# Projections of q and k made whole in every second batch, in place of halves in neighbouring batches

## The chip, the cores and the metric

The kernel runs on one core of one Trainium2 chip. The metric is the device time of one execution in microseconds; the time before is 4257.07 us, the median of 3 runs (4256.78 to 4263.16).

## The reference

The input is x of shape (8, 512, 32, 32): 8 images, 512 channels, 1024 tokens. Everything is fp32.

```python
def _mhsa(x, w_qkv, b_qkv, w_o, b_o):          # 8 heads of 64
    t = x.reshape(B, C, H * W).transpose(0, 2, 1)
    q, k, v = jnp.split(t @ w_qkv + b_qkv, 3, axis=-1)     # then split into heads
    scores = jnp.einsum('bhnd,bhmd->bhnm', q, k) / jnp.sqrt(jnp.float32(hd))
    out = jnp.einsum('bhnm,bhmd->bhnd', jax.nn.softmax(scores, axis=-1), v)
    return (out @ w_o + b_o)                   # back to (B, C, H, W)
def layer(x):                                  # x is the group norm of the input
    p = sigmoid(relu(mean(x, (2, 3)) @ w1 + b1) @ w2 + b2)
    m = (p > 0.5)[:, :, None, None]
    hyp = _logmap0(_mhsa(_expmap0(x * m), *hdn_weights))
    euc = _mhsa(x * (1 - m), *eu_weights)
    return hyp + euc
out = x + layer(_gn(x))
```

`_expmap0` and `_logmap0` scale each row of 32 numbers along the last axis by a function of its norm.

## The kernel before, in words

The kernel loops over the 8 images, and in each image over two passes, t = 0 (the first weight set, hdn) and t = 1 (the second, eu). A pass is the attention of four pairs of heads. It is cut into 32 batches of two steps each; a step is 128 keys of one pair against 512 queries. Five engines each walk through the same 32 batches in an order written out by hand, and wait for one another at semaphores that count what was made.

On TensorE, batch b is (lines 1284 to 1305): the maximum slot M0 (`max_slot`, two matmuls, L1184, into banks 0 and 1), the scores of two steps (`scores`, L1232, 16 matmuls in four parts each of high and low halves), the maximum slot M1, the products of the two steps before with v (`prob_v`, L1246), in batches 5, 9, 13, ... the denominators (`denominator`, L1256), in batches 7, 15, 23, 31 the negated row maxima turned by a matmul with the identity (`neg_rows`, L1193), and then `project(b)`: the projections that `projections(b)` (L103) lists for this batch. In pass 1, batches 2, 3, 5 and 6 have small tiles of the gate for the next image as well (`gate_tile`, L1142 to L1153); in batch 5 the one called hidden stands behind the projection and waits for a VectorE result (L968).

The maximum slots compute q times k of the next pair a second time, so that the row maxima of the softmax are known before its scores are. Both matmuls of a slot write banks 0 and 1, and VectorE reduces them (`max_slot` of VectorE, L1034, 128x1024). The next slot writes the same two banks, so M1 of a batch waits for the reduction of its M0, and M0 of the next batch for that of M1.

The projections make q and k of the pairs ahead. A tile (p, k) is one 128x512 half of q or k of pair p (p of 4 and 5 are pairs 0 and 1 of the next pass); it takes 12 matmuls L1135 (four blocks of channels, each high by high, high by low, low by high), accumulated in bank 2. `done` is the batch in which the tile gets complete: 4, 6, 8, ... 30, and 32 for the last two, which is the tail of the pass. Before the change, the first 6 matmuls stand in batch done - 1 and the other 6 in batch done; two tiles, (4, 0) in batch 20 and (5, 3) in batch 32, are whole. When a tile is complete, ScalarE writes its high part (`qk_hi`, L747) at the end of batch done, and VectorE its low part (`qk_lo`, L1023) in the batch behind, between its reductions of M0 and M1. v tiles (12 matmuls each) are made in batches 0 to 3, two in each, ahead of the tiles of q and k.

VectorE's order in batch b is (lines 1097 to 1113): the reduction of M0, the low part of the tile made in batch b - 1, the reduction of M1, then one half of a reciprocal of denominators (L1072, even batches from 6 to 30, and 31), in batches 11, 15, 19, 23, 27 and 31 the low part of the attention's output (`o_lo`, L1077), and `operand_step` (L961). That one has work in pass 1 alone (as has `y_scale_step` in its batches 0 to 2): statistics, norms of rows (L971), in batch 13 a chain of some 15 small operations on scales (L901 to L910 and others), and in batches 15 to 22 the multiply of a chunk of the next operand by its scales (L995), which waits for ScalarE's mask (L695).

GpSimd sums the probabilities of the steps (L640, 128x1024, seven in each eight steps), multiplies the output by the reciprocals (L647) and makes the low part of the next operand (L614). SyncE issues the loads; the weights w_qk of pair p for q or k are loaded once the last tile that reads the old ones is complete.

Of the kernel before, what the change touches and what calls it, by code (L numbers as in the profile page):

```python
# [18 lines left out]
PAIRS = HEADS // 2  # L19
# [83 lines left out]
def projections(b):  # L103

    out = [("v", m) for m in (2 * b, 2 * b + 1) if m < NT]
    for p in range(2, PAIRS + 2):
        for k in range(4):
            done = min(8 * p + QK_AT[k], BATCHES)

            first = done if (p, k) in ((PAIRS, 0), (PAIRS + 1, 3)) else done - 1  # L110
            out += [("qk", p, k, part) for part in range(2) if b == (first, done)[part]]
    return out


def made(b):

    return [f[:3] for f in projections(b) if f[0] == "v" or f[3]]
# [22 lines left out]
def aux_tiles(t):  # L140
# [18 lines left out]
    for b in range(BATCHES):  # L159
        for j in range(2):  # L160
            out += maxima(*max_slot_at(b, j))
        if phase_at(b, DEN) is not None:
            out += [((t, "den", phase_at(b, DEN)), "A", (1,))]
        if neg_pair(b) is not None:
            out += neg(neg_pair(b))
        gate = [((t, GATE_BATCH[b]), "D", (0,))] if t == 1 and b in GATE_BATCH else []
        if b != 5:
            out += gate
        for f in projections(b):
            if f[0] == "v":  # L170
                out += [((t,) + f, "A", (LAST_SCORE if f[1] % 2 else 1 if f[1] == 6 else 2,))]
            elif f[3]:
                out += [((t,) + f[:3], "Q", (2,))]
        if b == 5:
            out += gate
# [16 lines left out]
def build(nc, x, w1, b1, w2, b2, hw_qkv, hb_qkv, hw_o, hb_o, ew_qkv, eb_qkv, ew_o, eb_o, out):  # L192
    ctx = ExitStack()
    with ctx:
# [930 lines left out]
        def _(pe):  # L1125
# [82 lines left out]
            with pe.Fori(0, B) as i:  # L1208
                for t in range(2):
# [67 lines left out]
                    def project(b):  # L1277
                        for f in projections(b):
                            if f[0] == "qk":
                                qk_tile(i, t, f[1], f[2], (f[3],))  # L1280
                            else:
                                v_tile(f[1])
# [56 lines left out]
```

## Time and profile before

| | |
|---|---|
| median of 3 runs | 4257.07 us |
| the profiled execution | 4255.99 us, its span 4254.2 us |
| TensorE busy | 4027.7 us, 95% of the span, 21822 matmuls |
| VectorE busy | 2613.5 us, 61% |
| ScalarE busy | 1949.8 us, 46% |
| GpSimd busy | 2696.1 us, 63% |
| mean granted clock of TensorE | 0.982 |

The page gives the busy time of each engine and the chain of work that ended last. A wait on an engine that is not on that chain costs nothing. In the rows below PE is TensorE, DVE is VectorE, ACT ScalarE and POOL GpSimd; aux_ps holds banks 0 to 2.

### The profile page before, as it was taken

The numbers are of one execution on the slowest core, as the hardware profiler recorded it, in microseconds if no ns is written. First come the engines' busy times: TensorE is split into PE (matmuls) and PEld (weight loads), VectorE is DVE, ScalarE is ACT, GpSimd is POOL, SyncE is SP. The second block draws the span as 40 slices with busy tenths as digits, with TensorE's granted clock in tenths as the row PEclk, the third lists the DMA queues.
The fourth block names the chain that finished last, engine by engine and source line by source line (L and its number), as shares of the span: only waits on it lengthen the run. The fifth ranks groups of instructions, "written<-read, shape, count | busy, mean of one in ns | idle before, by whom it ended". The sixth has DMA issues, their size and how long they took to land.

```text
span 4254.2 us, 69112 instructions
## 1 busy us (share of the span) xinstructions
PE 4027.7 (95%) x21822; PEld 2420.4 (57%) x21822; DVE 2613.5 (61%) x2747; ACT 1949.8 (46%) x3520; POOL 2696.1 (63%) x1311
## 2 busy tenths in 40 slices
PE   4999899998999989998999999999899998999989
PEld 3556465564656546565565655656556564565645
DVE  5465845668465674667746577365763657646585
ACT  4454534545355443544535445354453544435353
POOL 4683766747675575755758458584585836858367
PEclk9999999999999999999999999999999999999999
DMA  7112131121211213121131211212112121121212
GB/s 264 65 41 95 53 100 45 48 96 42 95 55 57 91 33 110 41 77 65 39 104 45 82 55 51 93 53 75 57 61 85 53 88 46 62 90 41 92 51 85
DMA packets 143726, 306.49 MB, mean 72 GB/s; under 512 B 17248, under 2 KB 30048, under 8 KB 133088
## 3 DMA queue, kind: packets, MB, share of 16 engines
q1 hardware_dynamic: 143328, 301.53, 21.1%
q8 instruction: 207, 3.39, 0.3%
q14 instruction: 191, 1.56, 0.1%
HBM read 251.15 MB, written 50.33 MB: 71 GB/s over the span
## 4 chain that ended last, share of the span: by engine, by line
PE 84%; DVE 8%; issue 4%; DMA 2%; ACT 1%; POOL 0%; SPq 0%; DVEq 0%; ACTq 0%
PE aux_ps L1135 29%; PE acc_ps L1246 21%; PE score_ps L1232 20%; PE aux_ps L1184 8%; PE score_ps L1135 3%; PE aux_ps L1256 2%; DVE mxp L1034 2%; DMA xin<-in_x_dram 1%; DVE sc L902 1%; PE aux_ps L1193 1%; DVE sc L909 1%; DVE sc L910 0%; DVE small L903 0%; DVE sc L901 0%; DMA probs<-in_L_conv_eu_w_o_dram 0%
## 5 line engine op out<-in xcount | busy, mean ns | idle before, releaser
L640 POOL TENSOR_TENSOR sums<-sums,probs 128x1024 f32<-128x1024 f32 x768 | 1867.9, 2432 | 887.2 <-ACT probs L811 846.9
L1034 DVE TENSOR_REDUCE mxp<-aux_ps 128x2 f32<-128x1024 f32 x1031 | 1262.4, 1224 | 1204.0 <-PE aux_ps L1184 1192.8
L811 ACT ACTIVATE probs<-score_ps 128x512 f32<-128x512 f32 x2048 | 1057.2, 603 | 662.7 <-PE score_ps L1232 654.9
L1246 PE MATMUL acc_ps<-probs,v_y 128*64 128x512 f32 x4096 | 1015.9, 617 | 0.0
L1135 PE MATMUL aux_ps<-xs,w_qk 128*128 128x512 f32 x3072 | 835.4, 410 | 0.0
L1135 PEld LDWEIGHTS aux_ps<-xs,w_qk 128*128 128x128 f32 x3072 | 546.1, 189 | 412.1 <-issue 296.8
L640 POOL TENSOR_TENSOR sums<-probs 128x1024 f32<-128x1024 f32 x128 | 305.6, 2387 | 474.2 <-ACT probs L811 474.2
L1184 PE MATMUL aux_ps<-k_hi,q_hi 64*128 64x512 f32 x2062 | 474.2, 453 | 138.2 <-DVE mxp L1034 133.3
L1246 PEld LDWEIGHTS acc_ps<-probs,v_y 128*64 128x64 f32 x4096 | 252.0, 138 | 479.8 <-issue 442.1
L1072 DVE RECIPROCAL den<-den 128x256 f32<-128x256 f32 (+1 forms) x240 | 444.0, 1850 | 7.7 <-ACT den L822 7.7
L1232 PE MATMUL score_ps<-q_hi,k_hi 64*128 64x512 f32 x2048 | 408.5, 394 | 18.8 <-issue 18.8
L1184 PEld LDWEIGHTS aux_ps<-k_hi,q_hi 64*128 64x128 f32 x2062 | 199.1, 186 | 371.3 <-DVE mxp L1034 176.6
L1232 PE MATMUL score_ps<-q_hi,k_lo 64*128 64x512 f32 x2048 | 407.1, 393 | 0.0
L1232 PE MATMUL score_ps<-q_lo,k_hi 64*128 64x512 f32 x2048 | 406.8, 392 | 0.0
L1232 PE MATMUL score_ps<-q_max,first_row 64*128 64x512 f32 x2048 | 406.5, 392 | 0.0
L1135 PE MATMUL aux_ps<-o_t,w_o 128*128 128x512 f32 x1536 | 356.5, 391 | 0.2
L1135 PEld LDWEIGHTS aux_ps<-o_t,w_o 128*128 128x128 f32 x1536 | 286.4, 188 | 75.2 <-issue 16.3
L747 ACT ACTIVATE k_hi<-aux_ps,bias_q 128x512 fp32r<-128x512 f32 x128 | 88.1, 689 | 373.6 <-PE aux_ps L1135 373.6
L1077 DVE SCALAR_TENSOR_TENSOR o_t<-o_raw,bias_q,o_t 128x512 fp32r<-128x512 f32 x128 | 188.0, 1469 | 109.4 <-ACT o_t L827 109.4
L647 POOL TENSOR_TENSOR o_raw<-o_raw,den 128x512 f32<-128x512 f32 x128 | 169.5, 1324 | 133.1 <-DVE den L1072 133.1
L1232 PEld LDWEIGHTS score_ps<-q_hi,k_hi 64*128 64x128 f32 x2048 | 194.0, 186 | 47.8 <-issue 24.5
L1232 PEld LDWEIGHTS score_ps<-q_max,first_row 64*128 64x128 f32 x2048 | 195.3, 186 | 44.3
(142 smaller groups left out, 3441.9 us busy)
## 6 DMA issues: line engine op xcount, KB each, us to landing
w_qk<-w_split SPq DMA_DIRECT2D x130, 512.0 KB, 4.2
xin<-in_x_dram SPq DMA_DIRECT2D x256, 256.0 KB, 2.9
w_o<-w_split SPq DMA_DIRECT2D x32, 1024.0 KB, 7.2
w_v<-w_split SPq DMA_DIRECT2D x32, 1024.0 KB, 6.1
v_y<-in_x_dram SPq DMA_DIRECT2D x72, 256.0 KB, 2.9
y<-v_y SPq DMA_DIRECT2D x64, 256.0 KB, 2.0
xin<-y SPq DMA_DIRECT2D x64, 256.0 KB, 2.8
out_dram<-v_y SPq DMA_DIRECT2D x64, 256.0 KB, 7.1
```

The source lines that it names most:

```text
L640: pool.tensor_tensor(sums[h][:, :], a, probs[:, g % SLOTS_P, :], ALU.add).then_inc(c_sum[h].sem, 1)
L647: pool.tensor_tensor(o_raw[:, ph % 2, :], o_raw[:, ph % 2, :], den[:, ph % 2, :], ALU.mult).then_inc(c_on.sem, 1)
L747: act.activation((q_hi, k_hi)[what][:, p % 2, token_half(h)], ps, ACT.Identity, bias=bias_q[:, tt, what, pp:pp + 1]).then_inc(c_hi.sem, 1)
L811: act.activation(probs[:, n % SLOTS_P, token_half(u % 2)], score_ps[:, u % SCORE_BANKS, :], ACT.Exp, scale=SCALE).then_inc(c_exp.sem, 1)
L1034: dve.tensor_reduce(mxp[:, :, n, h], ps, AX.X, ALU.max).then_inc(c_free["D"].sem, 1)
L1072: dve.reciprocal(den[:, ph % 2, first:last], den[:, ph % 2, first:last]).then_inc(c_rec.sem, parts[1] - parts[0])
L1077: dve.scalar_tensor_tensor(o_t[:, 1, p, token_half(h)], o_raw[:, ph % 2, :], bias_q[:, t, 2, p:p + 1], o_t[:, 0, p, token_half(h)].bitcast ...
L1135: last = nc.tensor.matmul(ps, lhs(a, k), rhs(b, k), start=(j == 0), stop=(j == len(todo) - 1))
L1184: last = nc.tensor.matmul(ps[:, j, :], q_hi[head(j), p % 2, n * P:(n + 1) * P], k_hi[head(j), p % 2, token_half(h)], start=True, stop=True)
L1232: last = nc.tensor.matmul(score_ps[:, (2 * n + j) % SCORE_BANKS, :], lhs, qq[head(j), p % 2, cols], start=(s == 0), stop=(s == 3))
L1246: last = nc.tensor.matmul(acc_ps[head(j), :], v_y[:, m, head(2 * p + j)], probs[:, n % SLOTS_P, token_half(j)], start=(m == 0), stop=(m == ...
L1256: last = nc.tensor.matmul(ps[head(j), :], ones[:, :], sums[h][:, token_half(j)], start=True, stop=True)
```

## The change

The list of projections puts both halves of each tile of q and k into batch `done`. So batches 5, 7, 9, ... 31 and 3 hold no matmuls of q or k any more, and batches 4, 6, 8, ... 30 hold 12 of them in place of 6; the tail of the pass (batch 32) makes (5, 2) and (5, 3) whole. The tiles, their banks, the order in which they get complete, and all other engines' programs are as before.

```diff
@@ -106,8 +106,7 @@
     for p in range(2, PAIRS + 2):
         for k in range(4):
             done = min(8 * p + QK_AT[k], BATCHES)
-
-            first = done if (p, k) in ((PAIRS, 0), (PAIRS + 1, 3)) else done - 1
+            first = done
             out += [("qk", p, k, part) for part in range(2) if b == (first, done)[part]]
     return out
```

## Rows read from the trace of the kernel before

**Rows 1.** Section 4 of the page: shares of the chain that ended last, by engine.
```profile
PE 84%; DVE 8%; issue 4%; DMA 2%; ACT 1%; POOL 0%; SPq 0%; DVEq 0%; ACTq 0%
```

**Rows 2.** Waits of TensorE: who, for whom; us in total, times, longest.
```profile
PE aux_ps L1184 <- DVE mxp L1034: 133.3, 62, 8.6
```

**Rows 3.** Timeline (start, us, what) of TensorE, pass 0, end of batch 14, batch 15.
```profile
1240.84 1.67 PE L1135 MATMUL aux_ps<-xs,w_qk 128*128 128x512 f32 x6
1242.44 0.50 PE L1184 MATMUL aux_ps<-k_hi,q_hi 64*128 64x512 f32 x2
...
1244.62 0.39 PE L1184 MATMUL aux_ps<-k_hi,q_hi 64*128 64x512 f32 x2
...
1246.81 0.70 PE L1193 MATMUL aux_ps<-ident,mxw 128*65 128x128 f32 x8
1247.34 1.60 PE L1135 MATMUL aux_ps<-xs,w_qk 128*128 128x512 f32 x6
1248.87 0.50 PE L1184 MATMUL aux_ps<-k_hi,q_hi 64*128 64x512 f32 x2
```

**Rows 4.** The same of batches 19 and 20 and the start of batch 21.
```profile
1267.64 0.50 PE L1184 MATMUL aux_ps<-k_hi,q_hi 64*128 64x512 f32 x2
...
1272.00 0.50 PE L1184 MATMUL aux_ps<-k_hi,q_hi 64*128 64x512 f32 x2
...
1275.11 0.49 PE L1184 MATMUL aux_ps<-k_hi,q_hi 64*128 64x512 f32 x2 [0.74 <-DVE mxp L1034]
1275.53 1.94 PE L1246 MATMUL acc_ps<-probs,v_y 128*64 128x512 f32 x8
1277.40 3.01 PE L1135 MATMUL aux_ps<-xs,w_qk 128*128 128x512 f32 x12
1280.35 0.50 PE L1184 MATMUL aux_ps<-k_hi,q_hi 64*128 64x512 f32 x2
```

**Rows 5.** Timeline of VectorE, end of batch 19 and start of batch 20.
```profile
1271.39 2.44 DVE L1077 SCALAR_TENSOR_TENSOR o_t<-o_raw,bias_q,o_t 128x512 fp32r<-128x512 f32 x1
1273.75 1.21 DVE L1034 TENSOR_REDUCE mxp<-aux_ps 128x2 f32<-128x1024 f32 x1
```

**Rows 6.** Timeline of GpSimd in the same stretch.
```profile
1270.89 2.39 POOL L640 TENSOR_TENSOR sums<-sums,probs 128x1024 f32<-128x1024 f32 x1
```

**Rows 7.** Timelines of VectorE and TensorE, pass 1, batch 16 and what leads to it.
```profile
1517.51 1.21 DVE L1034 TENSOR_REDUCE mxp<-aux_ps 128x2 f32<-128x1024 f32 x1
...
1515.65 0.50 PE L1184 MATMUL aux_ps<-k_hi,q_hi 64*128 64x512 f32 x2
1518.87 0.49 PE L1184 MATMUL aux_ps<-k_hi,q_hi 64*128 64x512 f32 x2 [0.86 <-DVE mxp L1034]
```

**Rows 8.** Timeline of VectorE, pass 0, batch 11.
```profile
1221.49 1.87 DVE L1077 SCALAR_TENSOR_TENSOR o_t<-o_raw,bias_q,o_t 128x512 fp32r<-128x512 f32 x1
```

**Rows 9.** Windows of GpSimd, batches 17 to 19: window, us, busy (instructions), clock, DMA.
```profile
1257.55:1273.28 15.73, 15.57 (x8) 1.00 0.30 100
```

**Rows 10.** Timeline of TensorE, pass 1, the hidden gate tile in batch 5.
```profile
1439.36 0.82 PE L1150 MATMUL aux_ps<-small,xin 128*128 128x1 f32 x6 [1.17 <-DVE small L968]
```

**Rows 11.** Timeline of VectorE, pass 1, batches 11 and 12.
```profile
1477.15 2.42 DVE L1077 SCALAR_TENSOR_TENSOR o_t<-o_raw,bias_q,o_t 128x512 fp32r<-128x512 f32 x1
...
1480.09 1.21 DVE L1034 TENSOR_REDUCE mxp<-aux_ps 128x2 f32<-128x1024 f32 x1
```

**Rows 12.** Timeline of TensorE, pass 1, M1 of batch 14.
```profile
1503.18 0.80 PE L1184 MATMUL aux_ps<-k_hi,q_hi 64*128 64x512 f32 x2 [8.56 <-DVE mxp L1034]
```

**Rows 13.** Windows at clock 0.50: PE, PEld, DVE, ACT, POOL busy (instructions), clock, DMA.
```profile
405.28:408.69 3.41, 3.41 (x18) 2.35 (x16) 1.20 (x2) 1.84 (x4) 1.30 (x1) 0.50 0.21 71
4040.47:4043.88 3.41, 3.41 (x18) 2.04 (x16) 1.27 (x2) 1.95 (x4) 1.40 (x1) 0.50 0.22 68
```

**Rows 14.** Timeline of TensorE, pass 1, batch 20 of an image with such a stretch.
```profile
1544.60 3.00 PE L1246 MATMUL acc_ps<-probs,v_y 128*64 128x512 f32 x8
1547.53 3.56 PE L1135 MATMUL aux_ps<-xs,w_qk 128*128 128x512 f32 x12
```

## The prediction

> **What bounds the kernel now.** I read the page first: TensorE holds 84% of the chain that ended last [rows 1]. So its own matmul time counts, and so does each wait that it takes. The waits of TensorE come next [rows 2]: 133.3 us in 62 waits are for the row maxima (VectorE's reduction L1034, which frees the two banks of a maximum slot). Then I read the timeline of single batches. A batch here is: maximum slot "M0", 16 score matmuls, maximum slot "M1", the two products with v, and the projection matmuls. Times behind a T are counted from the start of the batch's M0; even and odd mean the batch number; pass 0 and pass 1 are the two weight sets of one image.
>
> A plain batch with half a tile: the half begins at 1240.84 and the next M0 at 1242.44, so a half costs 1.60 us [rows 3]. Batch 19 of pass 0 has no projection even now (tile (4, 0) is whole in batch 20): it lasts from 1267.64 to 1272.00, 4.36 us. Batch 20 has the whole tile, 1277.40 to 1280.35, 2.95 us [rows 4]. A plain batch of today is thus 4.36 + 1.60 = 5.96. In batch 20 M1 starts 3.11 us behind M0 and not 2.18 (1242.44 to 1244.62 [rows 3]), with an idle of 0.74 put down to the maxima [rows 4]. Why: VectorE's o_lo (L1077) begins at 1271.39, 3.75 us into batch 19, takes 2.44, and only then comes the reduction of batch 20's M0, 1.75 us into that batch [rows 5]. GpSimd's sum runs from 1270.89 to 1273.28 and the o_lo ends 0.55 behind it [rows 5, 6]. So this is the one place that shows the kernel as it will be: an odd batch without projection, followed by a whole tile.
>
> Its length gives the price of a late reduction: 8.35 (1272.00 to 1280.35) less 2.18 + 2.19 + 2.95 = 7.32 for the undisturbed one (2.19 is M1 to the end of what follows it, 1244.62 to 1246.81 [rows 3]) is 1.03, with the reduction at 1.75. I use: delay = start of M0's reduction - 0.72, if that is over 0.1. Check: in batch 16 of pass 1 the reduction starts at 1517.51 - 1515.65 = 1.86, which gives 1.14; the M1 at 1518.87 is 3.22 behind M0, 1.04 over the 2.18, and the refill of 0.1 behind it is the rest [rows 7].
>
> **The change, part by part.** No instruction is added or removed. In 14 of the 16 tiles of a pass, 6 matmuls go from the odd batch into the even one behind it.
>
> *TensorE's own time.* The odd batch loses 1.60, the even one gains 2.95 - 1.60 = 1.35: 0.25 less per pair, the price of one visit to the full array between the others. Nine pairs of a pass are plain or have a denominator in the odd batch (its fp32 matmuls stand ahead of the projection as the products with v do). In batches 7, 15, 23 and 31 the negated maxima (L1193) stand before the half, which then costs 1.53 (1247.34 to 1248.87 [rows 3]). What L1193 costs directly ahead of M0 no row shows. Bounds: no price (then 1.35 - 1.53 = -0.18 for the pair), and the 0.25 of a whole visit (+0.07). The half's own last step into M0 is a part of such a visit, so I take a value between, 0.08: -0.10 a pair, and an odd batch of 6.43 - 1.53 + 0.08 = 4.98 (6.43 is 1242.44 to 1248.87). In batch 3 the half follows v tiles, also full-array work: -0.02.
> The Trainium skill, "TensorEngine Tiling (Array Packing)", Key Properties, says that changing the tiling mode drains the array. By it a visit has a price of its own, as the 0.25 here shows, and the maxima of batches 7 to 31 keep theirs; without the rule these pairs would save 0.25 too, 0.15 x 7 x 8 = 8 us less in the sum.
>
> *What hides under the half now and then does not.* VectorE's work behind M1 has until the next M0 plus 0.8 us. In a plain odd batch that limit comes down from 5.96 to 4.36.
>
> Pass 0. Batches 11 and 27 have an o_lo of 1.87 from 1221.49 [rows 8], 3.75 into the batch, so the next reduction can start at 5.54 (records overlap by 0.08 [rows 5]): 5.54 - 4.36 - 0.72 = 0.46 each. Batch 23 has the long o_lo of 2.44 as batch 19 has, a little later for batch 23's two short reductions more (free at 6.14): 6.14 - 4.98 - 0.72 = 0.44. Batch 15's ends in time. From batch 17 to the end of that sum in batch 19 GpSimd is busy 15.57 of 15.73 us [rows 9], and so from batch 21 to 23: its absolute times stay while the batch begins 0.25 earlier, +0.25 in both. Pass 0: stalls 0.46 x 2 + 0.44 + 0.50 = 1.86; TensorE's own 9 x 0.25 + 3 x 0.10 + 0.10 (batches 31 and 3) = 2.65 less. Net -0.8.
>
> Pass 1 has the work on the next image as well.
> - Batches 5/6: the hidden gate tile waits 1.17 us for VectorE (L968) behind the half [rows 10]. Its start is set by VectorE, so the half comes out from under it: batch 5 gains nothing, batch 6 grows by 1.35, a wait at batch 7 goes in the images that have it (0.2 on the mean): +1.15.
> - Batches 11/12: after the o_lo a reduction of squares, M0's starts at 1480.09, 2.94 behind the o_lo's 1477.15 and so 3.75 + 2.94 = 6.69 into batch 11 [rows 11]. 6.69 - 4.36 - 0.72 = 1.61, less 0.25, less 0.12 that batch 13 is late now: +1.25.
> - Batches 13/14: TensorE waits 8.56 for the chain of scale operations [rows 12]. The chain starts at M1 of batch 13 and is as long as before: the wait is 10.2 and the pair +1.35.
> - Batches 15/16: the operand's multiply (L995) puts the reduction at 8.29 from batch 15's M0 wherever batch 16 begins [rows 7]: +1.35.
> - Batches 19/20: unchanged but for the shift of 0.25. Batches 27/28: a stall of 0.46.
> - Plain pairs: six at -0.25 (9, 17, 21, 25, 27, 29), four small ones -0.3 in all.
> Pass 1: 1.15 + 1.25 + 1.35 + 1.35 + 0.25 + 0.46 - 1.5 - 0.3 = +4.0.
>
> One image: 4.0 - 0.8 = 3.2; eight: +26 us.
>
> *The clock.* It is granted at 0.50 (1.2 GHz of 2.4) for 3.41 us at a time in 15 places of the loop ([rows 13] are the first and the last), for twice that in one, and for longer around each of the eight waits in batch 14 of pass 1. What such a stretch costs shows in batch 20 of pass 1: the products take 3.00 in place of 1.94 and the whole tile 3.56 in place of 3.01 [rows 4, 14], together 1.6. It follows a wait of 1.9 in 3 images of 8 there, and comes in 5 of 8 at batch 6 behind the gate's waits. The waits get longer at batch 5 (1.2 to 2.8), 12 (0 to 1.5) and 16 (0.9 to 2.4). No row has these waits. Bounds: none more (0), and one in each image at each place, 3 + 8 + 8 = 19 (30 us). I take 8 (3 at batch 6, 4 at 16, 1 at 12), 13 us.
>
> *What costs nothing.* The weights' loads wait for the end of the tiles two steps before, in the same batches as now, and their readers come one batch later or the same; SP's queue holds nothing longer. ScalarE's and VectorE's reads of the tiles stand in the same even batch's tail and the batch behind, in the same order. In the tail of a pass the first matmul behind the last projection keeps its place, 1.6 earlier and 1.6 longer.
>
> Sum: 26 + 13 = 39 on the profiled 4255.99 (span 4254.2 and 1.8 around it), 4295; the median of the runs is 1.1 higher, and GpSimd's escape (below) pulls a little: I take 4294.
>
> The Trainium skill, "SBUF — State Buffer", in "SBUF: two separate sides", says that GpSimd and a VectorE operation with two SBUF inputs lock one another out for a whole instruction. By it the o_lo of batch 19 would run its 0.75 after the sum; the trace has 0.55 [rows 5, 6] (0.75 is what it takes in batch 23 of pass 1, clear of any sum). With the rule's whole wait some six stalls of an image would be 0.2 longer, +10 us, a time of 4304; I give it no more than the trace does.
>
> **The rivals.**
> 1. *Only TensorE's own work counts* (faster). If the reductions never come late, 2.65 in each pass is saved: 5.3 x 8 = 42 less, 4215. For it: TensorE has 84% of the chain. Against: batch 20 of pass 0 stalls today exactly so. It decides for the other sign where VectorE's work behind M1 ends before about 5.1 in a plain odd batch; rows 11 and 7 have it at 6.7 and 8.3. Chance 6%.
> 2. *GpSimd slips behind the o_lo.* In batches 19 and 23 of pass 0 the sum starts 3.25 to 3.3 in and the o_lo 3.75. With the shift of 0.25 there is 0.2 left; if the sum starts behind the o_lo, that one takes some 0.75 and the stalls of 1.29 and 0.69 go: -2.0 x 8 = -16, 4278. Chance 18%.
> 3. *The clock doesn't notice*: no further stretch at 0.50, 4281. Chance 14%.
> 4. *The clock falls at each longer wait*: 19 more, 4311. Chance 14%.
> 5. *It comes out even*: 2 and 3 together, 26 - 16 = 10, and a visit saved in the batches of the maxima too, -8: 4259. Chance 6%.
>
> **How the numbers follow.** My forecast has 42%. What a measurement of this kernel can tell from no change is about 0.2%, 8.5 us. Slower by more: the forecast and 2 to 4 less 3% where two of them meet, 85%. Within: 5 and 2 of those, 8%. Faster: the first and 1 of them, 7%. The range of 4262 to 4316 has the bounds of the clock (0 and 30) and of the maxima's batches (0.28 + 0.10 in place of -0.10, x 6 x 8 = 18 over what I took; 0.08 x 6 x 8 = 4 under it), and leaves out the first rival and the far corner where all goes wrong.
>
> **What would show it.** Odd plain batches of 4.36 us and whole tiles of 2.95 everywhere. Idle before L1184 put down to the maxima up from 133 to about 133 + 8 x (1.5 + 1.6 + 1.6 in pass 1's batches 12, 14, 16, and some 2.0 in the small ones) = 187 us; the longest such wait 10.2. The wait of L1150 in batch 5 up from 1.2 to 2.8. TensorE's busy time down by the 42 us of the visits, up by what the clock costs. Wrong would be: batch 16 of pass 1 with a wait under 2 us, batch 14's still 8.6, or a batch behind an odd one with a stall that I have not named.

## The result and the profile after

The changed kernel takes 4425.76 us (median of 4 runs, 4418.91 to 4430.97) against 4256.92 us before: a ratio of 1.0393 (95% interval 1.0375 to 1.0412). I had forecast 4294, slower by 0.9%, in a range of 4262 to 4316. The sign is right; the loss is more than four times as large. The profiled execution has a span of 4429.1 us, 175 more than before, at a mean granted clock of 0.974 in place of 0.982.

The page first, the busy time of TensorE (time, share, matmuls) and the shares of the chain:

```profile
PE 4037.2 (91%) x21822; PEld 2463.3 (56%) x21822; DVE 2637.1 (60%) x2747; ACT 1949.3 (44%) x3520; POOL 2688.3 (61%) x1311
...
PE 76%; DVE 10%; issue 8%; POOL 2%; ACT 2%; DMA 1%; DVEq 0%; ACTq 0%; SPq 0%; POOLq 0%
```

TensorE has the same matmuls and hardly more busy time; its share of the chain fell from 84% [rows 1] to 76%. So the loss is in waits. The waits of TensorE in the changed kernel (who, for whom; us in total, times, longest; all lines are one lower than before from L109 on):

```profile
PE aux_ps L1183 <- DVE mxp L1033: 168.1, 91, 9.4
PE aux_ps L1183 <- ACT den L821: 72.5, 104, 0.7
PE aux_ps L1183 <- ACT q_max L752: 45.9, 49, 1.0
...
PE aux_ps L1149 <- DVE small L967: 21.6, 8, 2.7
```

The first is the one that I had priced, up from 133.3 [rows 2] (187 forecast). The second did not exist before the change, and of the third there was one wait of 0.8 us: before a maximum slot, TensorE now waits for ScalarE's copy of the denominators (L821) and of the negated row maxima (L752). Batches 9 and 10 of pass 0 show it, TensorE first, then ScalarE (`...` stands for rows left out):

```profile
1256.93 0.51 PE L1183 MATMUL aux_ps<-k_hi,q_hi 64*128 64x512 f32 x2
...
1259.44 1.94 PE L1245 MATMUL acc_ps<-probs,v_y 128*64 128x512 f32 x8
1261.21 1.03 PE L1255 MATMUL aux_ps<-sums,ones 128*64 128x512 f32 x4
1262.93 0.50 PE L1183 MATMUL aux_ps<-k_hi,q_hi 64*128 64x512 f32 x2 [0.70 <-ACT den L821]
...
1267.33 3.03 PE L1134 MATMUL aux_ps<-xs,w_qk 128*128 128x512 f32 x12
1270.29 0.50 PE L1183 MATMUL aux_ps<-k_hi,q_hi 64*128 64x512 f32 x2
```

```profile
1262.28 0.60 ACT L821 ACTIVATE den<-aux_ps 128x512 f32<-128x512 f32 x1 [1.83 <-PE aux_ps L1255]
```

The denominators are written to bank 1. ScalarE copies them out from 1262.28 to 1262.88, and M0 of batch 10, which writes banks 0 and 1, starts at 1262.93. Batch 9 lasts 6.00 us and not 5.22 (6.82 less a half of 1.60). Before the change the half stood in bank 2 between the two and covered the copy. The negated maxima are the same case, with two copies, out of banks 0 and 1 (batch 7 of pass 0, TensorE, then ScalarE):

```profile
1247.95 0.70 PE L1192 MATMUL aux_ps<-ident,mxw 128*65 128x128 f32 x8
1249.58 0.50 PE L1183 MATMUL aux_ps<-k_hi,q_hi 64*128 64x512 f32 x2 [0.93 <-ACT q_max L752]
```

```profile
1248.45 1.08 ACT L752 ACTIVATE q_max<-aux_ps 65x512 fp32r<-65x512 f32 x2 [1.36 <-PE aux_ps L1192]
```

The next M0 starts 1.63 us behind the start of the maxima's matmuls here; with the half between them it was 0.53 + 1.53 = 2.06 [rows 3]. So the odd batch gets 0.43 us shorter where I had counted on 1.45.

The lengths of the batches, from the start of one M0 to the next, as means over the 8 images:

```
                      before              changed
pass 0, batch 9+10    6.82 + 5.97         6.01 + 7.34    +0.56   (7 such pairs)
pass 0, batch 7+8     6.43 + 5.97         6.01 + 7.37    +0.98   (3)
pass 0, batch 11+12   5.96 + 5.97         4.39 + 7.78    +0.24
pass 0, batch 27+28   5.96 + 5.97         4.39 + 7.75    +0.21
pass 0, batch 19+20   4.36 + 8.35         4.39 + 8.12    -0.20
pass 1, batch 5+6     9.50 + 7.82         10.04 + 10.05  +2.77
pass 1, batch 11..14  36.18               38.46          +2.28
pass 1, batch 15+16   13.53               14.87          +1.34
pass 1, batch 19+20   14.47               17.43          +2.96
whole pass 0 / 1      246.4 / 272.5       254.1 / 286.8  +7.8 / +14.2
```

Eight images at 22.0 are the 175 us, within rounding. The 12 pairs behind a denominator that nothing else holds (pass 1's batches 6 and 14 wait for VectorE anyway) make 12 x 0.56 = 6.7, the five pairs of maxima 4.9 (the sixth, batches 15 and 16 of pass 1, waits for VectorE anyway).

The third loss stands in batch 20 of pass 1. VectorE, GpSimd and TensorE there (batch 19 begins at 1599.29, batch 20 at 1603.68):

```profile
1603.06 2.50 DVE L1076 SCALAR_TENSOR_TENSOR o_t<-o_raw,bias_q,o_t 128x512 fp32r<-128x512 f32 x1
1605.49 2.84 DVE L994 TENSOR_TENSOR xin<-xin,sc 128x512 f32<-128x512 f32 x1
1608.25 1.21 DVE L1033 TENSOR_REDUCE mxp<-aux_ps 128x2 f32<-128x1024 f32 x1
```

```profile
1602.65 5.13 POOL L639 TENSOR_TENSOR sums<-sums,probs 128x1024 f32<-128x1024 f32 x2
```

```profile
1609.62 0.80 PE L1183 MATMUL aux_ps<-k_hi,q_hi 64*128 64x512 f32 x2 [3.59 <-DVE mxp L1033]
1610.34 3.68 PE L1245 MATMUL acc_ps<-probs,v_y 128*64 128x512 f32 x8
1613.95 3.78 PE L1134 MATMUL aux_ps<-xs,w_qk 128*128 128x512 f32 x12
```

GpSimd's two sums run from 1602.65 to 1607.78. The o_lo, 0.75 us when no GpSimd instruction runs beside it, takes 2.50, and the multiply, 0.68 at its shortest in this trace, takes 2.84. The reduction of M0 starts 4.57 us into the batch and M1 waits 3.59. Before the change the same M1 waited 1.9:

```profile
1544.17 0.50 PE L1184 MATMUL aux_ps<-k_hi,q_hi 64*128 64x512 f32 x2 [1.92 <-DVE mxp L1034]
```

Behind the wait the products take 3.68 us at a granted clock of 0.50, in place of 1.94 at full clock [rows 4].

### The profile page after: what moved, and what is told of

Same layout as the page of the kernel before. It is cut to its first block, busy times and chain, and to the rows that moved or that the text cites. A ratio compares the mean times of both kernels' runs of the same rounds, so it can differ in the third digit from the quotient of the medians.

```text
span 4429.1 us, 69112 instructions
## 1 busy us (share of the span) xinstructions
PE 4037.2 (91%) x21822; PEld 2463.3 (56%) x21822; DVE 2637.1 (60%) x2747; ACT 1949.3 (44%) x3520; POOL 2688.3 (61%) x1311
## 3 DMA queue, kind: packets, MB, share of 16 engines
q1 hardware_dynamic: 143328, 301.53, 20.1%
## 4 chain that ended last, share of the span: by engine, by line
PE 76%; DVE 10%; issue 8%; POOL 2%; ACT 2%; DMA 1%; DVEq 0%; ACTq 0%; SPq 0%; POOLq 0%
PE aux_ps L1134 27%; PE acc_ps L1245 18%; PE score_ps L1231 17%; PE aux_ps L1183 7%; PE score_ps L1134 3%; DVE mxp L1033 3%; PE aux_ps L1255 2%; POOL sums L639 2%; ACT den L821 1%; DVE o_t L1076 1%; DMA xin<-in_x_dram 1%; DVE sc L901 1%; DVE xin L994 1%; DVE sc L908 1%; ACT q_max L752 1%
## 5 line engine op out<-in xcount | busy, mean ns | idle before, releaser
L1134 PE MATMUL aux_ps<-xs,w_qk 128*128 128x512 f32 x3072 | 773.5, 401 | 0.0
L1134 PEld LDWEIGHTS aux_ps<-xs,w_qk 128*128 128x128 f32 x3072 | 560.4, 189 | 309.3 <-issue 184.5
L1076 DVE SCALAR_TENSOR_TENSOR o_t<-o_raw,bias_q,o_t 128x512 fp32r<-128x512 f32 x128 | 204.5, 1597 | 109.0 <-ACT o_t L826 109.0
L746 ACT ACTIVATE q_hi<-aux_ps,bias_q 128x512 fp32r<-128x512 f32 x132 | 90.9, 688 | 308.6 <-PE aux_ps L1134 308.6
```

The costliest lines, as they stand in the source:

```text
L746: act.activation((q_hi, k_hi)[what][:, p % 2, token_half(h)], ps, ACT.Identity, bias=bias_q[:, tt, what, pp:pp + 1]).then_inc(c_hi.sem, 1)
L1076: dve.scalar_tensor_tensor(o_t[:, 1, p, token_half(h)], o_raw[:, ph % 2, :], bias_q[:, t, 2, p:p + 1], o_t[:, 0, p, token_half(h)].bitcast ...
L1134: last = nc.tensor.matmul(ps, lhs(a, k), rhs(b, k), start=(j == 0), stop=(j == len(todo) - 1))
```

## The experiments

Theory A: the half covered ScalarE's copies out of the banks of the next maximum slot. Its rival B: the short batches crowd ScalarE or VectorE, and the wait would show at any bank.

Each ratio below is to the kernel before, run in the same set: its median was 4255.28 us beside the first three experiments and the better kernel, 4261.93 beside the mirror and the plain batches, 4262.79 beside the other four, and 4256.92 beside the changed kernel. So a difference in us between kernels of two sets can be some 6 us off. Line numbers move by up to three from kernel to kernel with the lines that an edit adds.

**Denominators in another bank.** The changed kernel with

```diff
-            out += [((t, "den", phase_at(b, DEN)), "A", (1,))]
+            out += [((t, "den", phase_at(b, DEN)), "A", (2,))]
```

> The changed kernel, with the denominators of phases 0 to 6 in bank 2 in place of bank 1. Theory A (the lost cover is the time in which ScalarE copies a small tile out of the banks that M0 needs next): the waits of L1183 on the copy of den go (72.5 us, 104 times) and the 0.09 or so that hangs on each; 12 batches in an image get 0.79 shorter, 12 x 0.79 x 8 = 76 us less than the changed kernel's 4426, so 4350, a ratio of 1.022 to the kernel before. The waits on the negated maxima (45.9 us) stay. Theory B (TensorE is held by work that got crowded on ScalarE or VectorE in the short batches, whatever the bank): the time stays at 4426, and the same wait shows under another name.

Measured: 4330.55 us, ratio 1.0176 (1.0160 to 1.0191), 95 us less than the changed kernel. The wait on the copy of den is gone from the list, that of the maxima is there as before:

```profile
PE aux_ps L1183 <- DVE mxp L1033: 162.9, 88, 10.2
PE aux_ps L1183 <- ACT q_max L752: 46.1, 49, 1.0
```

```profile
1231.05 1.03 PE L1255 MATMUL aux_ps<-sums,ones 128*64 128x512 f32 x4
1232.01 0.50 PE L1183 MATMUL aux_ps<-k_hi,q_hi 64*128 64x512 f32 x2
...
1234.17 0.40 PE L1183 MATMUL aux_ps<-k_hi,q_hi 64*128 64x512 f32 x2
```

M0 stands 0.96 us behind the start of the denominators and not 1.72. Theory B falls: only the bank was changed, and the wait is gone. Pass 1's batch 20 went from 13.04 to 9.68 us on the mean, which is 27 us and more than the rest of the 95 over the 76. Two places gave some of it back: batch 14 of pass 1 is 1.3 longer (its M1 waits 0.77 more, because batch 13 in front of it is that much shorter and VectorE's chain is not; the rest comes with longer stretches at clock 0.50), and batch 20 of pass 0 is 0.46 longer.

**Whole tiles only behind denominators, in the kernel before.**

```diff
-            first = done if (p, k) in ((PAIRS, 0), (PAIRS + 1, 3)) else done - 1
+            first = done if (p, k) in ((PAIRS, 0), (PAIRS + 1, 3)) or done in (10, 18, 22, 26, 30) else done - 1
```

> The kernel before, with tiles made whole only where the odd batch holds a denominator (even batches 10, 18, 22, 26, 30). Theory A: each such pair costs 0.79 for the copy out of bank 1 and saves 0.25 of TensorE's own: +0.54 x 5 x 2 x 8 = +43 us, and up to 3 x 8 = 24 more if the wait of pass 1's batch 20 (1.9 before, 3.6 after the change) comes from batch 17 losing its half: 4300 to 4324. The prediction's sum for these pairs was -0.25 x 80 = -20 us: 4237.

Measured: 4322.73 us, ratio 1.0158 (1.0143 to 1.0174). That is 67 us more than before. The wait is there in just the 80 places (43 us at the expected 0.54 each), and pass 1's batch 20 lasts 14.0 us in place of 10.1 (31 us; smaller places give some back):

```profile
PE aux_ps L1184 <- ACT den L822: 55.8, 80, 0.7
```

**Whole tiles only behind the negated maxima** (the same edit with `done in (8, 16, 24)`).

> The kernel before, with tiles made whole only where the odd batch holds the negated row maxima (even batches 8, 16, 24). Theory A: M0 needs bank 0 and bank 1 and waits for ScalarE's second copy: 13.38 us for the two batches in place of 12.40, so +0.97 for five of the six pairs of an image and +1.35 for pass 1's batches 15 and 16, where VectorE's late reduction hides it: 6.2 x 8 = +50 us, 4307. The prediction's sum was -0.10 x 5 and +0.44 and +1.35: +10 us, 4267.

Measured: 4298.0 us, ratio 1.0104 (1.0088 to 1.0119): 43 us more than before where 50 were expected and 10 by the prediction's sum. Batches 7 and 8 of pass 0 last 5.98 + 7.35. The wait for the copies is 45.8 us in 49 places, as in the changed kernel.

**The mirror: halves kept, denominators in bank 2.** The kernel before with the first experiment's edit. Nothing is merged; the half itself now needs the bank.

> The kernel before, halves and all, with the denominators of phases 0 to 6 in bank 2 in place of bank 1. Here the half that stands right behind them needs bank 2, so nothing covers ScalarE's copy. Theory A: the same 0.79 us that the changed kernel pays at bank 1 is paid here before the half, in 7 batches of pass 0 and in 5 or 6 of pass 1 (batch 13 is held by VectorE): 12 x 0.77 x 8 = +74 us, and up to 24 more if batch 20 of pass 1 gets its long wait from it: 4330 to 4355, ratio 1.018 to 1.023. Theory B (the wait came from whole tiles crowding the other engines): the time stays at that of the kernel before.

Measured: 4351.72 us, ratio 1.0214 (1.0196 to 1.0231).

```profile
PE aux_ps L1135 <- ACT den L822: 78.1, 112, 0.7
```

```profile
1238.11 1.03 PE L1256 MATMUL aux_ps<-sums,ones 128*64 128x512 f32 x4
1239.83 1.65 PE L1135 MATMUL aux_ps<-xs,w_qk 128*128 128x512 f32 x6 [0.70 <-ACT den L822]
```

The same 0.70 of idle with halves in every batch. It is thus no matter of whole or half: whoever first needs the bank behind the small tile pays for the copy. Besides the 12 pairs, batches 19, 20 and 23 of pass 1 got longer, by 1.40, 0.96 and 1.33 us, each with a longer or a new wait of its M1 for VectorE.

**One of the maxima's two banks given back.** The changed kernel, the denominators in bank 2, and

```diff
-        return [((t, "neg", p, h), "A", (h,)) for h in range(2)]
+        return [((t, "neg", p, h), "A", (2 * h if t >= 0 else h,)) for h in range(2)]
```

> The changed kernel with the denominators in bank 2 (the first experiment's) and, besides, the second half of the negated row maxima in bank 2 in place of bank 1. Theory A: M0 of batches 8, 16 and 24 waits for the first of ScalarE's two copies alone, which ends 0.5 us before the second; the odd batches 7, 15, 23 get 5.5 us in place of 6.01. Five of the six in an image gain (pass 1's batch 16 is held by VectorE): 5 x 0.5 x 8 = 20 us under the first experiment's 4331, so 4311, ratio 1.013. Theory B' (M0 waits for neg as such, the bank does not matter): 4331.

Measured: 4330.49 us, ratio 1.0160 (1.0145 to 1.0175), not told apart from the first experiment's 1.0176 (the intervals overlap). The 20 us did not come: the ratios differ by 0.0016 (7 us), the spans of the traces by 3 us. The trace has the first step as expected and a second one that I had not seen (batches 7 and 8 of pass 0):

```profile
1216.34 0.70 PE L1192 MATMUL aux_ps<-ident,mxw 128*65 128x128 f32 x8
1217.48 0.51 PE L1183 MATMUL aux_ps<-k_hi,q_hi 64*128 64x512 f32 x2 [0.44 <-ACT q_max L752]
1218.04 0.50 PE L1231 MATMUL score_ps<-q_hi,k_hi 64*128 64x512 f32 x2
```

M0 is 1.14 us behind the maxima's start and no longer 1.63; but the scores of batch 8 are the first of a new pair and wait for both copies, since the maxima are an operand of theirs. They start 0.56 behind M0 and not 0.33. Batch 7 lasts 5.53, batch 8 7.68: together 0.17 less than in the changed kernel. The second copy is needed at that time as data, not only as a bank.

**VectorE's late work, pass 1.** The changed kernel with halves given back in pass 1 to batches 6, 12, 14 and 16:

```diff
+HALVES = [(), (6, 12, 14, 16)]
-            first = done
+            first = done - 1 if done in HALVES[t] else done
```

> The changed kernel, with the halves given back in pass 1 where VectorE's work for the next image is late (even batches 6, 12, 14, 16). The prediction's own terms for these were 1.15 + 1.25 + 1.35 + 1.35 = 5.1 us in an image; read from the changed kernel's trace they are 2.1 + 2.3 + 1.3 = 5.7 with what the clock added, so -41 to -46 us: 4382, ratio 1.029. If these waits are independent of the half above them, the time stays at 4426.

Measured: 4380.43 us, ratio 1.0281 (1.0264 to 1.0298), 45 us less (48 by the ratios). Batches 11 to 14 are at 36.2 us again, 15 and 16 at 13.5, and 5 and 6 at 17.1, where the changed kernel has 20.1: these two give the largest part, 3.0 of some 6.6 us in an image.

**Plain batches alone.** The kernel before with `done in (12, 28)` whole.

> The kernel before, with tiles whole only in batches 12 and 28, behind plain odd batches with VectorE's o_lo. By the prediction's price (start of the reduction less 0.72, less 0.25 for the visit): 0.21 x 3 + 1.36 less 0.12 in an image, +15 us, ratio 1.0035; the changed kernel's trace has 0.24, 0.21, 0.21 and 1.36 for these pairs. If o_lo was not what holds them, -8 us.

Measured: 4278.17 us, ratio 1.0036 (1.0024 to 1.0049), where 1.0035 was expected. Batches 11 and 12 last 4.36 + 7.78 in pass 0 and 4.36 + 8.94 in pass 1, as in the changed kernel. The price of a late reduction (its start less 0.72) holds. This run shows the price of the clock as well: M1 of pass 1's batch 20 waits 1.9 as before the change, but the granted clock is 0.50 behind it in all eight images and not in three. The batch lasts 11.1 us in each of them; before the change it lasted 9.5 in the five images without such a stretch.

**Batch 20 of pass 1.** The changed kernel with `HALVES = [(), (18,)]`: one pair, batches 17 and 18 of pass 1.

> The changed kernel, with the halves given back to one pair alone: batches 17 and 18 of pass 1. Theory: batch 20 of pass 1 waits 3.6 us in place of 1.9 because batch 17 ends 0.8 late for bank 1, GpSimd (which works without a pause) is by then ahead of VectorE, begins its sum before o_lo, and locks first o_lo and then the operand's multiply out, each to the end of a sum. With the halves back, batch 19 begins where it did before: o_lo takes 0.75 again, batch 20's wait is 1.9. Batches 17 to 20 from 30.8 to 27.3: -28 us, 4398, ratio 1.033. Rival: the wait of batch 20 has grown by the clock or by the longer batch 16 ahead; then only 0.54 x 8 = 4 us go.

Measured: 4395.49 us, ratio 1.0315 (1.0300 to 1.0331), 30 us less (33 by the ratios) for 8 halves moved. Batch 20 lasts 9.68 us, and its M1 waits 1.9 again. GpSimd and VectorE in batch 19 (it begins at 1586.54):

```profile
1589.22 1.29 POOL L616 TENSOR_TENSOR xs<-xin,xs 128x512 fp32r<-128x512 f32 x1
1590.46 5.62 POOL L642 TENSOR_TENSOR sums<-sums,probs 128x1024 f32<-128x1024 f32 x2
```

```profile
1590.29 0.76 DVE L1079 SCALAR_TENSOR_TENSOR o_t<-o_raw,bias_q,o_t 128x512 fp32r<-128x512 f32 x1
1591.14 2.71 DVE L997 TENSOR_TENSOR xin<-xin,sc 128x512 f32<-128x512 f32 x1
1593.78 1.21 DVE L1036 TENSOR_REDUCE mxp<-aux_ps 128x2 f32<-128x1024 f32 x1
```

Here the o_lo starts 0.17 before the sum and takes 0.76; in the changed kernel the sum started 0.41 before it, and it took 2.50. The rival (the clock, the longer batch 16) is out as the cause of the longer wait: batch 16 is as in the changed kernel, 8.87. The clock is part of the gain all the same: one image of eight has a stretch at 0.50 in batch 20, where all eight had one.

**A better kernel.** Whole tiles only where neither engine needs the cover, with the denominators of just these batches in bank 2, from the kernel before:

```diff
+WHOLE = [(6, 10, 14, 18, 22, 26, 30), (10, 22, 26, 30)]
-            first = done if (p, k) in ((PAIRS, 0), (PAIRS + 1, 3)) else done - 1
+            first = done if (p, k) in ((PAIRS, 0), (PAIRS + 1, 3)) or done in WHOLE[t] else done - 1
-            out += [((t, "den", phase_at(b, DEN)), "A", (1,))]
+            out += [((t, "den", phase_at(b, DEN)), "A", (2 if b + 1 in WHOLE[t] else 1,))]
```

> The kernel before, with tiles whole only where nothing under the half needs its cover once the denominators of these batches are in bank 2: pass 0 even batches 6, 10, 14, 18, 22, 26, 30, pass 1 10, 22, 26, 30. Theory A: 11 pairs at -0.25 in an image, 22 us: 4235, ratio 0.995, with no new wait anywhere. If a visit to the full array costs nothing of its own (the 0.25 was a matter of the stalled batch in which it was read), the time is that of the kernel before, 4257.

Measured: 4238.13 us (5 runs), ratio 0.9964 (0.9951 to 0.9978). TensorE's list of waits has only the old ones:

```profile
PE aux_ps L1187 <- DVE mxp L1037: 133.8, 57, 8.6
```

Batches 9 and 10 of pass 0 last 5.23 + 7.32, 0.24 less than before. The gain is small, 0.36%, but its interval lies below 1. The 22 us expected lie just beyond the interval (9 to 21): batch 20 of pass 0 gave 2 of them back, 8.59 in place of 8.35, the 0.25 that the prediction had for its earlier start. With pass 1's batch 18 in the list as well:

> The better kernel of the fourth experiment, with pass 1's batch 18 whole as well and its denominator in bank 2. In the first experiment batches 17 to 20 of pass 1 took 26.6 us together, before the change 27.3: -0.6 x 8 = -5 us, 4233, ratio 0.9952. If the wait of batch 20 grows to 3.6 as it did in the changed kernel, +14 us, 4252.

Measured: 4240.03 us (6 runs), ratio 0.9950 (0.9938 to 0.9962). It beats the kernel before too; the two are not told apart, their intervals overlap. Batch 20 does not get the long wait (10.5 us).

## Why the prediction was wrong, point by point

- *What hides under the half.* This is the step that failed. The prediction took VectorE's work for all that the half covers and wrote of ScalarE's reads only those of the q and k tiles, under "What costs nothing". The copies of the denominators and the maxima out of banks 0 and 1 are not in it: it put that term at nothing. What the runs showed in its place: they cost 0.77 us in 12 batches of an image and, for the maxima, 1.08 more than counted in five: 9.2 + 5.4 = 14.6 us of the 22.0 in an image, 117 us in all. The experiments on the banks (76 expected, 95 measured, with batch 20's share), on the denominators alone and the mirror show the first; that on the maxima alone shows the second. With these 117, the 22 that batches 19 and 20 of pass 1 took beyond their term, and the forecast's own 39 (13 of them for the clock), the sum is 178 us for the 175 measured.
- *The plain pairs of pass 0 and 1* came as priced: 0.21 forecast, 0.24 and 0.21 measured.
- *Pass 1, batches 11 to 16*: 1.25 + 1.35 + 1.35 = 3.95 forecast, 2.28 + 1.34 = 3.62 measured. M1 of batch 14 waits 9.4 and M0 of it 0.70 (the copy), together the 10.1 that I had put at 10.2. In batch 16 M1 waits 1.27 us and not 2.4. A wait under 2 there was one of my own signs of being wrong, and it says the same thing: M0 of batch 16 stands 1.03 later than counted, behind the copies of the maxima, and takes that much out of the wait for VectorE. The other sign came too, stalls behind odd batches that I had not named.
- *Pass 1, batches 5 and 6*: +1.15 forecast, +2.77 measured. The gate's wait came as priced, 2.7 (2.8 forecast). The rest goes along with a lower clock: a stretch at 0.50 stands in all eight images there, in six of them 6.83 us long, where five had one of 3.41. No run separates it from the wait.
- *Batches 19 and 20 of pass 1*: +0.25 forecast, +2.96 measured, of which 1.7 is the longer wait of M1 and most of the rest the clock. I had weighed a small slip of GpSimd against the o_lo, and only to the better side, in pass 0. The slip came the other way, made by the missed wait of batch 17 (0.77 us): 24 us for the two batches, and the experiment with one pair takes them back.
- *The visit to the full array*: 0.25 a pair. The better kernel saves 0.24 a pair in the trace and 15 us in time (22 expected, 9 to 21 by the interval). What the maxima's matmuls cost directly ahead of M0 (my 0.08) stays unmeasured: in every run without the half there, M0 waits for the copies.
- *The clock*: 8 more stretches at 0.50 forecast. The mean granted clock fell from 0.982 to 0.974 in the profiled runs (0.974 to 0.978 in all four), batch 20 of pass 1 is slowed in all images and not in three, batch 5 or 6 in all and not in five. Batches 12 and 16 of pass 1, where I had put five of the eight, have none behind waits of 1.3 us. Such a stretch costs 1.6 us in batch 20 (the run with plain batches alone). What it costs over all, no run separates.
- *Rival 2* (GpSimd behind the o_lo in pass 0) did not come: batch 20 of pass 0 still waits 0.54. *Rival 1* fell: the time went up.

## What to carry to other kernels

When work is moved from between two users of a buffer, list each writer and reader of every bank that the next instruction needs, on all engines. A reader that nobody was ever seen to wait for may be the one that was covered. To find it in a trace, take the instruction that will come next after the change and look up when each thing that it waits for was last done. And a filler between two dependent steps is worth more than the switch it costs: here 0.77 against 0.25.

## What the runs showed of the hardware

- A visit of the 128-row projection between the 64-row score matmuls costs 0.25 us over its matmuls (1.60 for six, 2.95 for twelve). It does so where nothing waits too: with one visit in place of two, batches 9 and 10 of pass 0 went from 12.79 to 12.55 us in the better kernel.
- Which of GpSimd and VectorE starts first decides the length of a VectorE operation on two SBUF operands: 0.76 us when it starts 0.17 ahead of GpSimd's sum, 2.50 when it starts 0.41 behind. In the changed kernel each of the 96 o_lo's that start while a GpSimd instruction runs ends 0.55 us behind that one's end. With the denominators in bank 2 batch 17 of pass 1 is 0.77 us shorter than in the changed kernel, and M1 of batch 20, three batches later, waits 2.1 us and not 3.6.
- Behind the same wait of 1.9 us in batch 20 of pass 1 the granted clock fell to 0.50 in three images of eight in the kernel before and in eight of eight in the kernel with the plain batches whole; behind waits of 1.3 us in batches 12 and 16 it never fell in the changed kernel.
